# SP's loop of the two edge stages cut to the block loads; ACT issues tables, flags and stores of sums

## The reference, cut to what matters

```python
h = (x @ W.T).reshape(n, H, D)                      # 8 heads of 32
alpha = einsum(h[src], a_src) + einsum(h[dst], a_dst)
enc = relu(edge_attr @ edge_W.T + edge_b).reshape(-1, H, D)
alpha = leaky(alpha + sum(enc * h[dst], axis=-1))
ex = exp(alpha - segment_max(alpha, dst)[dst])
attn = ex / segment_sum(ex, dst)[dst]
out = segment_sum(h[src] * attn[..., None], dst) + bias
```

## Time and profile before

| | us |
|---|---|
| median of 3 runs | 6683.05 (6675.22 to 6683.12) |
| profiled execution, its own time (span) | 7807.0 |
| edge stage of layer 0, stretch 405 to 3120 of the profile | 2715 |
| edge stage of layer 1, stretch 4640 to 7150 | 2510 |

### The profile page before, as it was taken

The page is one execution under the profiler, slowest core; times in us unless marked ns, Lnnn a source line. Parts: engine busy times, 40 slices in busy tenths (PEclk is TensorE's granted clock), DMA queues, the critical chain, the costliest instruction groups (busy, mean ns, idle before and its releaser), DMA issues. The chain is left out here.

```text
span 7807.0 us, 99204 instructions
## 1 busy us (share of the span) xinstructions
PE 5257.7 (67%) x19729; PEld 3739.4 (48%) x19729; DVE 3278.9 (42%) x5938; ACT 1371.0 (18%) x2977; POOL 3613.4 (46%) x3708
## 2 busy tenths in 40 slices
PE   2387887788788878228999625556565556663498
PEld 1144444444444444227999514444444444442498
DVE  6255555555555555721111313333333333336244
ACT  2122222222222222002222200000000000000122
POOL 2635555555555554042222056666666666650222
PEclk9689999999999999658999857777777777786699
DMA  6434444444444443515666544444444444434255
GB/s 220 136 101 122 122 119 123 124 124 125 122 123 121 122 124 102 186 60 165 183 183 183 153 102 114 113 115 115 114 112 113 113 114 116 113 102 154 101 198 188
DMA packets 718013, 1022.24 MB, mean 131 GB/s; under 512 B 301733, under 2 KB 531561, under 8 KB 692608
## 3 DMA queue, kind: packets, MB, share of 16 engines
q0 software_dynamic: 183456, 485.95, 23.8%
q1 hardware_dynamic: 527676, 519.31, 21.7%
q10 hardware_dynamic: 6564, 14.14, 0.5%
HBM read 868.26 MB, written 153.27 MB: 131 GB/s over the span
## 5 line engine op out<-in xcount | busy, mean ns | idle before, releaser
L773 POOL DMA_INDIRECT e_rows<-sc_table,e_eidx x3224 | 3115.9, 966 | 2253.8 <-issue 952.6
L880 PE MATMUL e_ps_o<-e_rows,e_oh 128*128 128x264 f32 x6448 | 1918.5, 449 | 856.9 <-ACT e_res L969 700.8
L880 PEld LDWEIGHTS e_ps_o<-e_rows,e_oh 128*128 128x128 f32 x6448 | 1379.2, 222 | 1384.3 <-issue 1147.6
L1064 DVE SCALAR_TENSOR_TENSOR e_u<-e_encr,e_adst,e_ps_hd 128x512 f32<-128x512 f32 x806 | 597.1, 745 | 1160.2 <-remote 366.1
L1132 DVE TENSOR_TENSOR e_rows<-e_rows,e_ps_w 128x1024 f32<-128x1024 f32 x806 | 970.7, 1207 | 106.3 <-issue 83.5
L822 PE MATMUL e_ps_X<-e_u,e_hwide 128*104 128x512 f32 x1612 | 871.1, 635 | 16.8 <-DVE e_u L1064 14.8
L1055 DVE TENSOR_SCALAR e_ohT<-e_at,e_nid 96x512 bf16<-96x512 int16 x806 | 292.5, 363 | 1384.6 <-DMA e_aw<-sc_a2p 553.7
L969 ACT COPY e_res<-e_ps_o 32x264 f32<-32x264 f32 x806 | 296.0, 367 | 3291.4 <-PE e_ps_o L884 1242.4
L810 PE MATMUL e_ps_enc<-e_at,e_w_enc 96*128 96x512 bf16 x806 | 317.9, 394 | 570.6 <-ACT e_encr L942 383.4
L1676 PE MATMUL x_ps_h<-x_xT,x_w 128*128 128x256 f32 x2624 | 648.2, 405 | 15.4 <-DMA x_b<-in_L_ffn_b_dram 15.4
L1676 PEld LDWEIGHTS x_ps_h<-x_xT,x_w 128*128 128x128 f32 x2624 | 638.5, 337 | 20.6 <-issue 16.4
(11 more groups left out here) (290 smaller groups left out, 3538.7 us busy)
## 6 DMA issues: line engine op xcount, KB each, us to landing
x_w<-in_L_ffn_W_dram SPq DMA_DIRECT2D x112, 1024.0 KB
e_at<-sc_grp SPq DMA_DIRECT2D x403, 192.0 KB
x_w<-in_L_ffn_w_dram SPq DMA_DIRECT2D x60, 1024.0 KB
e_rows<-sc_table,e_eidx POOLq DMA_INDIRECT x3224
e_at<-sc_grp SPq DMA_DIRECT2D x403, 96.0 KB
sc_agg<-e_res SPq DMA_DIRECT2D x816, 33.0 KB
sc_xb<-r_zero SPq DMA_DIRECT2D x24, 1032.0 KB
x_xin<-sc_xb SPq DMA_DIRECT2D x86, 258.0 KB
```

The source lines that it names most:

```text
L773: pool.indirect_dma_start(rows[:, k, s, j, :], None, dr["table"][:, :], bass.IndirectOffsetOnAxis(eidx[:, k, s, j:j + 1], 0)).then_inc(s_r ...
L880: nc.tensor.matmul(ps_o[:, 0:ROW], oh[:, k, at_j:at_j + P], rows[:, k, s, j, :], start=(j == 0), stop=False)
L1064: nc.vector.scalar_tensor_tensor(u[:, p, h, :], encr[:, h, :], adst[:, h:h + 1], ps_hd[:, h, :], ALU.add, ALU.mult).then_inc(s_u, 1)
```

## The change

SP keeps only the block loads, in one loop over batches of 13 blocks, from the first block on; its wait for a free ring slot uses the same semaphores with a head start (`F0`) so that one form fits all blocks. An entry read on SP is two words instead of three. ACT issues the tables (after s = 3 of a phase), the flags (after s = 9), and each block's store, one block after its eviction and ahead of that block's relu in program order. ACT reads one word for a store. The wait of `evict` for its slot is gone. DVE's waits change only by the head start.

```diff
+        F0 = SB * (2 if first else 1)
+        s_fre = s_hd if first else s_xa
...
-        def since(s):
-            return SB - KEEP if s < KEEP else KEEP if s < 2 * KEEP else SB
...
+        def tables(eng, t, k):
...
+        def flags(eng, t, k):
...
-                _, vals = nc.values_load_multi_w_load_instructions(tab[0:1, bass.ds(t * 3, 3)], engines=[sp.engine], min_val=0, max_val=NP,
+                _, vals = nc.values_load_multi_w_load_instructions(tab[0:1, bass.ds(t * 3, 2)], engines=[sp.engine], min_val=0, max_val=NP,
...
-            def store(t, s, n):
-                hold(sp, s_out, t * 16 - (32 * SB - OUT0), s_ps)
-                hold(sp, s_ev, t - (BEHIND - 1 - EV0), s_ps)
-                sp.dma_start(dr["agg"][bass.ds(n, WIN), :], res[0:WIN, kept((s - BEHIND) % SB), :]).then_inc(s_out, 16)
+            def fetch(b, s):
+                t = b * SB + s
+                hold(sp, s_fre, t * PER - (behind(s) - 1) * PER + F0, s_ps)
+                g, n = entry(t)
+                load(ring(s), g, n)
...
+            sp.sem_inc(s_fre, F0)
             steps = steps_of(sp)
-            def phase(b, k):
...
+            with sp.Fori(0, steps * 2 + 3) as b:
                 for s in range(SB):
-                    t = b * SB + (2 * SB + s)
...
+                    fetch(b, s)
...
         @block.scalar
...
+            def next_tables(b, k):
+                hold(act, s_dn, b * 2 + 2, s_pa)
+                tables(act, (b + 2) * SB, k)
+
+            def next_flags(b, k):
+                flags(act, (b + 2) * SB, k)
...
             def evict(b, s):
                 t = b * SB + s
                 hold(act, s_o, t + (1 + O0), s_pa)
-                if not isinstance(t, int) or t + BEHIND - 2 * SB + 1 >= since(s):
-                    hold(act, s_out, t * 16 + 16 * (BEHIND - 2 * SB + 2 - since(s)), s_pa)
                 nc.scalar.copy(res[0:WIN, kept(s), :], ps_o[0:WIN, 0:ROW]).then_inc(s_ev, 1)
+
+            def window(t):
...
+                _, vals = nc.values_load_multi_w_load_instructions(tab[0:1, bass.ds(t * 3 + 1, 1)], engines=[act.engine], min_val=0, max_val=NP,
...
+            def store(b, s):
+                t = b * SB + s
+                hold(act, s_out, t * 16 + OUT0, s_pa)
+                hold(act, s_ev, t + (1 + EV0), s_pa)
+                act.dma_start(dr["agg"][bass.ds(window(t), WIN), :], res[0:WIN, kept(s), :]).then_inc(s_out, 16)
...
                 for s in range(SB):
                     evict(b, s)
+                    if s > 0:
+                        store(b, s - 1)
+                    elif not isinstance(b, int) or b > 0:
+                        store(b - 1, SB - 1)
                     if first and pre:
                         relu(n, s)
                     if turn and s == 1:
                         sources(m, 1 - k, turns)
                         leak(m)
+                    if pre and s == 3:
+                        next_tables(m, 1 - k)
                     if turn and s == 6:
                         fade(m)
                     if turn and s == 9:
                         power(m)
+                    if pre and s == 9:
+                        next_flags(m, 1 - k)
                     if turn and s == 10:
                         place(m, 1 - k)
```

More of the change, by code:

```diff
@@ L652, in steps_of @@
             return eng.value_load(nbi[0:1, 0:1], min_val=1, max_val=MAXSTEP)
+        def tables(eng, t, k):
+            with nc.allow_non_contiguous_dma(reason="an edge's numbers go to the partition that its row goes to"):
+                eng.dma_start(eidx[:, k, :, :], dr["eslot"][bass.ds(t, SB), :, :].rearrange("t p c -> p t c")).then_inc(s_ei[k], 16)
+            eng.dma_start(ns[:, k, :], dr["nsf"][bass.ds(t, SB + 1)].partition_broadcast(P)).then_inc(s_ns[k], 16)
+        def flags(eng, t, k):
+            eng.dma_start(fr[:, k, :], dr["rec"][bass.ds(t, SB), :].unsqueeze(1).to_broadcast([SB, HEADS, REC])).then_inc(s_fr[k], 16)
+            eng.dma_start(link[0:1, k, 0:HEADS * LINKS].rearrange("a (h x) -> a h x", h=HEADS)[:, :, 1:LINKS - 1],
+                         dr["flg"][bass.ds(t, SB), :].rearrange("(a t) c -> a (t c)", a=1).unsqueeze(1).to_broadcast([1, HEADS, 2 * SB])
+                         ).then_inc(s_fr[k], 16)
         block = ctx.enter_context(nc.Block())
@@ L699, in _ @@
             sp.wait_ge(s_ready, 1)
             for b in range(2):
[L701 to L718, removed]
@@ L719, in _ @@
-            sp.sem_inc(s_out, OUT0)
+                tables(sp, b * SB, b)
+                flags(sp, b * SB, b)
+            sp.sem_inc(s_fre, F0)
             steps = steps_of(sp)
-            def phase(b, k):
+            with sp.Fori(0, steps * 2 + 3) as b:
                 for s in range(SB):
-                    t = b * SB + (2 * SB + s)
[L725 to L747, removed]
+                    fetch(b, s)
@@ L936, in _ @@
             act.sem_inc(s_ev, EV0)
+            if first:
+                act.wait_ge(s_wp, 1)
+                for k in range(3):
+                    for i in range(3):
+                        act.dma_start(w_enc[12 * k + 4 * i:12 * k + 4 * i + 4, :], w_part[:, k, :]).then_inc(s_we, 16)
+            def next_tables(b, k):
[3 more added lines that the diff above has]
+                flags(act, (b + 2) * SB, k)
             def relu(b, s):
@@ L966, in evict @@
                 hold(act, s_o, t + (1 + O0), s_pa)
-                if not isinstance(t, int) or t + BEHIND - 2 * SB + 1 >= since(s):
-                    hold(act, s_out, t * 16 + 16 * (BEHIND - 2 * SB + 2 - since(s)), s_pa)
                 nc.scalar.copy(res[0:WIN, kept(s), :], ps_o[0:WIN, 0:ROW]).then_inc(s_ev, 1)
+            def window(t):
+                why = "the planning stage writes only starts of windows that lie inside their arrays"
+                _, vals = nc.values_load_multi_w_load_instructions(tab[0:1, bass.ds(t * 3 + 1, 1)], engines=[act.engine], min_val=0, max_val=NP,
+                                                                   skip_runtime_bounds_check_because=why)
+                return nc.s_assert_within(vals[0], 0, NP, skip_runtime_bounds_check_because=why)
+            def store(b, s):
[3 more added lines that the diff above has]
+                act.dma_start(dr["agg"][bass.ds(window(t), WIN), :], res[0:WIN, kept(s), :]).then_inc(s_out, 16)
             def phase(b, k, pre, turn, turns):
@@ L991, in _ @@
             leak(0)
+            next_tables(0, 0)
             fade(0)
             power(0)
+            next_flags(0, 0)
             place(0, 0)
@@ L997, in _ @@
                     relu(1, s)
+            act.sem_inc(s_out, OUT0)
             steps = steps_of(act)
@@ L1004, in _ @@
             phase(steps * 2 + 2, 0, False, False, 0)
+            store(steps * 2 + 2, SB - 1)
+            hold(act, s_out, steps * (32 * SB) + (48 * SB + OUT0), s_pa)
+            hold(act, s_ei[1], steps * 16 + 32, s_pa)
+            hold(act, s_ns[1], steps * 16 + 32, s_pa)
+            hold(act, s_fr[1], steps * 32 + 64, s_pa)
         @block.vector
```

13 lines of the change are left out of this document (2 added, 11 removed).

## The result

| | before | after |
|---|---|---|
| median | 6681.52 us (6675.22 to 6683.12, 4 runs) | 7065.90 us (7053.87 to 7077.43, 4 runs) |
| profiled execution, its span | 7807.0 us | 7052.1 us |
| layer 0, first gather to last eviction | 2934.8 us | 2658.7 us |
| layer 1, the same | 2588.1 us | 2109.2 us |

The change makes the kernel slower: ratio 1.058, 95% interval 1.0566 to 1.0593, or 384 us. That is the forecast (7020) in direction and, within 46 us, in size.

What follows compares the result with a forecast made beforehand. Untraced, POOL's pace was taken to bound layer 1 and about PE's layer 0, the median 200 us above POOL's floor. 6683 + 415 - 35 - 40 = 7023, called 7020 us; 8 in 10 from 6600 to 7200.

Steps and rivals of the forecast that it cites:

- The choice to distrust the first profile: Both edge stages: most traced waits are stretched by tracing; removing a wait gives back at most 200 us untraced.
- against the profiled execution's own time: Whole kernel: second sum, starting from the traced 7807.0 us instead of the median, giving 8037 us.
- Part 1: Layer 0, ACT: the store ahead of relu delays it 1.1 us in 377 blocks, costing 415 us (226 to 566).
- Part 2: Layer 0: slack where POOL rather than PE sets a block absorbs 35 us of the delay.
- Part 3: ACT issuing tables and flags behind both relus: fits before PE's next need, taken as 0.
- Part 4: Layer 1: the store on ACT fits in the turn between evictions, cost 0.
- Part 5: SP relieved of stores: fewer late loads and waits, worth 40 us untraced, at most 200.
- Part 6: The rest: removing evict's wait saves 0.15 us, hidden by PE's finish; SP's loop and weights' loads 0 within 10 us.
- A: SP's lateness is real untraced and its relief decides: faster, 6560 us, at best 6483; chance 0.19.
- B: ACT's store hidden behind the score and SP not late, nearly cancelling: no change, 6683 us; chance 0.06.
- C: Both layers: a store's landing outlasts a block, ACT holds the eviction and PE stops; 7206 us; chance 0.12.
- The signs: Profile marks expected after the change: layer 0's relu gap, block length and waits grow; layer 1's load and store waits shrink.

Runs made afterwards that it cites:

- experiment 1: The changed kernel with each store on ACT moved behind both relus of the turn instead of ahead of them: 6683.98 us.
- experiment 2: The changed kernel with each store on ACT moved between the relu of h = 0 and that of h = 1: 6628.59 us.
- experiment 6: The kernel before with two or six already met waits added on ACT between eviction and relus, layer 0 only: 6705.12 and 6838.76 us.
- experiment 5: The kernel before with only tables and flags moved to ACT at the changed kernel's places, stores staying on SP: 6683.15 us.
- experiment 3: Layer 0's edge stage as in the kernel before, layer 1's as in the changed kernel: 6682.26 us.
- experiment 7: The kernel of experiment 2 with one met wait put back ahead of each eviction's copy in layer 0: 6660.90 us.
- experiment 10: The changed kernel with four more already met waits ahead of each store in layer 0: 7276.83 us.
- experiment 8: No run of its own: a reading of the profile of experiment 1 (6683.98 us) against that of experiment 2 (6628.59 us).

## Why the prediction was right, and which steps failed

The sum came within 46 us of the median because its large term was right. Of the small ones two were not there (-35 and -40), one was put at nothing and was worth -53, and a loss of 37 in the turns with softmax steps had no term: 400 - 53 + 37 = 384 measured, against 415 - 35 - 40 = 340. That these errors left the total so near is partly luck.

**The choice to distrust the first profile: right.** The rest of the program, the stages at POOL's and PE's pace, and a layer 1 at 2112 us against the floor of 2097 are all in the undisturbed profile. The reason given for it, that tracing stretches the waits, does not hold: the later execution was traced too and is not stretched. What stretched the first one stays open. The sum "against the profiled execution's own time", 8037, had nothing to stand on: after's execution was 7052.1.

**Part 1, the store ahead of relu: right.** Forecast 1.1 us on each of 377 blocks, 415 us. Measured 1.335 - 0.275 = 1.06, so 400. Experiments 1 and 2 remove it by its place alone, experiment 6 makes a loss of the same kind without a store, in proportion to the delay. One reading beside it was wrong: that PE's second L810 starts just when the score before it lets it, and so that 4.95 us is PE's own pace. In experiment 2 the second L770 starts at 2005.62, 0.16 us before the end that the profile gives for the score (2004.76 + 1.02), and the block takes 4.82. The pace before was that of the loop from PE's last matmul over eviction and relu back to PE. The one-word read that carried the choice is 0.28 us on ACT:

```profile
L943 ACTq TENSOR_LOAD <-e_tab x806: 272/280/535, 373.7 to 6330.5; - x162
```

The Trainium skill, page "DMA: Bandwidth & Descriptors", section "Latency and other measured facts", has about 600 ns as a floor for it. These 806 reads disagree, and the estimate by that figure, a term 120 us larger (535), would have missed the 400.

**Part 2, slack of 35 us: not there.** Experiment 6 loses the full delay already at 0.07 us. Thirteen blocks take PE and ACT 71.3 us before, and POOL's gathers 13 x 5.00 = 65, so POOL sets no block there over a batch.

**Part 3, tables and flags 0: right** in after's order (experiment 5); behind the store of experiment 1 the turn with the flags is 0.6 us longer. **Part 4, stores in layer 1 at 0: right** (experiment 3).

**Part 5, SP relieved, -40: wrong, it is 0.** Experiment 3 has the relief in layer 1 and gains nothing; in layer 0, experiment 7 and its timelines put all but 3 of the 54 us that experiment 2 gained down to the removed wait. The 512.4 and 348.3 us of waits belonged to the stretched execution and to POOL's pace. The rule that the prediction weighed here, of the Trainium skill, page "DMA: Bandwidth & Descriptors", section "Issuing engines are not separate DMA queues", lets such a move save the sequencer's time alone. Experiment 3 agrees: 6682.3 against 6683.0 us.

**Part 6: the step that failed.** "Removing `evict`'s wait saves 0.15 us ahead of each eviction on ACT, which PE's finish hides." The 0.15 was right (0.27 - 0.12, experiment 7) and the hiding was not: what stands ahead of the eviction also stands ahead of relu h = 0, the path that part 1 had called without slack. It was worth 0.14 us a block, 53 us (experiments 2 and 7). The same argument ought to have been applied to both.

Together: 5.87 = 4.95 + 1.06 - 0.14 for the even block. 377 x 0.92 = 347. The thirteen turns sum to 84.53 us after and 71.30 before, 29 x 13.23 = 384. What is above 347 falls mainly in the turns s = 0 and s = 1, longer by 1.54 and 1.83 us instead of 0.92; there the clock stood at its lower level for 160 us in all, against 51 before. At half pace that would be up to 55 us, an estimate; the prediction had no term for it.

**The rivals.** A (SP's lateness decides) and B (cancelled) fall with experiments 1 and 3. C (a landing holds ACT): its waits came, 260.4 us in layer 1, but where POOL sets the pace; in layer 0 of after no wait for `sc_agg` is among the waits at all. **The signs:** eviction to relu 1.35 (told 1.4), the block 5.87 (told 6.0), a wait in nearly every block (372), POOL's waits for PE in layer 0 (106.2 to 508.9), no wait of DVE for `e_aw`, and layer 1 no longer than before: as told. PE's wait for relu was to be 500 or more and is 385.1, as it was added to a stretched execution's 268; and layer 1's waits for `sc_agg` did not vanish, since the store carries a wait of its own.

## What to carry to other kernels

Issuing a transfer on a computing engine costs that engine's sequencer the waits, the register read and the issue, here 1.06 us, before the next instruction in its order may start; ACT is busy 698 of 2659 us in layer 0 and still has nothing to spare at that one place. Put the issue where the engine waits anyway: between the two relus it moved the second by 0.02 us, and the kernel took 437 us less than with the store ahead of them. And before you read waits from a profile, hold its span beside the timed median; where they differ by a sixth, profile it again.

## What the hardware showed that was not expected

- **A wait that is already met costs ACT 0.08 to 0.10 us** (0.081 each in experiment 6, 0.393 / 4 = 0.098 in experiment 10, 0.10 in experiment 7); the one taken from `evict`, which also works out its value, 0.15.
- **After a wait PE may compute at half the clock, and the wait's length alone does not say whether.** In the two turns shown in experiment 8, after PE's idle 2.31 us the eight matmuls of L840 took 3.57 us, and after 1.90 us of idle 1.95. The granted clock of the two stretches:

```profile
2026.00:2029.30 3.30, 3.30 (x10) 2.56 (x9) 2.08 (x3) 0.60 (x1) 1.61 (x2) 0.52 0.60 183
2097.20:2099.00 1.80, 1.80 (x11) 1.54 (x10) 0.80 (x2) 0.60 (x1) 1.50 (x2) 1.00 0.88 220
```

  The first ran nearly all at the lower of the two levels, 1.2 GHz (0.50), the second at the upper, 2.4 GHz (1.00). But the pair is not a rule. Of the 29 such turns of experiment 1, all 14 with 2.3 us of idle had some of the lower level in these matmuls (2.48 to 3.73 us), and of the 14 with 1.9 us 9 had it too (3.00 to 3.62) and 5 had not. In before, 28 such turns had 1.07 us of idle each, and it came in 14 of them.
- **A profiled execution can be 17% longer than the timed ones** (7807.0 against 6683) and a later one of the same program not (6672.4).
